# Mixture-of-experts tiles of 128 rows instead of 256, with the first weight matrices kept on chip

## The chip, the cores and the metric

The kernel runs on one core of a Trainium2 chip. The metric is the device time of one execution in microseconds (us). A kernel's time is the median of several runs. A change of under 0.3% (6.3 us here) can't be told from none.

## The reference, cut to what matters

x has 16 sequences of 256 rows with 128 channels, 4096 rows in all. A convolution with linear attention, two layers with one expert per row and three attention layers surround two calls of the layer that is changed here. `_L1_ffn_ref` picks, for each row, the two best of E = 8 experts and adds their weighted outputs:

```
xn = layernorm(x) * gamma + beta
probs = softmax(xn @ Wr + br)
scores, idx = top_k(probs, 2)
full[e] = relu(xn @ W1[e] + b1[e]) @ W2[e] + b2[e]      # W1: 128 x 512, W2: 512 x 128
sel_full = full[idx]
c[e] = relu(b1[e]) @ W2[e] + b2[e];  c_sel = c[idx];  c_total = sum of c over e
output = sum over the two of scores * (sel_full - c_sel + c_total)
return x + output
```

Everything is 32-bit floating point. The constant c_total - c_sel is prepared once, and is what a tile adds with its output.

## The kernel before, in words

The phases run one after the other: `conv_phase`, `linear_phase`, `ffn_phase`, `moe0_phase`, attention a0, `moe0_phase`, attention a1, `sparse_phase` "m1a", attention a2, `sparse_phase` "m1b". Only the sparse phases compute the layer above, each on two halves of 2048 rows (HALF = 16 blocks of P = 128 rows).

**Routing.** `routing` makes, for each half, the places of the rows sorted by expert. Each row occurs twice, so a half has 4096 rows. Each expert's rows fill tiles of SLOTS rows of their own. SLOTS is 256, MOST = 8, and TILES = 2 * MOST + E - 1 = 23 tiles are always computed. `te` holds the expert of each tile. The first half is routed inside the attention phase before. The second half is routed in the first tiles of the sparse phase, by the functions `aside` of each engine: normalised rows by ScalarE (`scaled`, L2345), transposes on TensorE (`turn_rows`), `take_rows` (L2368), `logits` (L2375), VectorE's `residual` (L2355), `biased`, `choose` (L2386 to L2429), `count` and `place` (L2466 to L2498), and `exps` (L2434). `scatter` (L2506) then writes rows to their places in DRAM by 32 indirect DMAs on POOL, of 128 rows each.

**A tile.** `sparse_phase` has Q = 46 tiles, with these steps:

- SP loads the rows (`load_rows`, L2606) and one expert's row of the DRAM table `wtab`. That row has WROW = 512 + 4 + 128 elements per partition: W1, b1 and the constant. `load` (L2614) reads the expert's number from `te` into a register (`value_load`, L2612) and puts it in the address. Both have rings of RING = 4.
- TensorE transposes the rows (`turn_in`, helper `turn`, L82), and ScalarE copies them out, scaled by gamma and beta (`take_in`, L2863).
- TensorE multiplies by W1 (`up`, L2821): four matmuls of 256 columns, in two pairs (semaphores up0 and up1). It reads the expert's number too (L2814).
- ScalarE takes the first pair through bias and relu (`relu`, L2870), VectorE the second (L2711).
- TensorE multiplies by W2 (`down`, L2832): eight matmuls of 128 columns into the single bank DN. W2e for all experts is on chip.
- VectorE adds the constant (`take_out`, L2719, semaphore y), and SP stores the tile (`store`, L2619).

A 32-bit matmul shows as two records in the trace, so `up` has 8 records and `down` 16. A transpose shows as one record.

**The order of the work** is written out by hand. On TensorE iteration q is up(q+1), turn_in(q+2), down(q), aside(q). down(q) waits for y of tile q-1, up(q+1) for xT of q+1, its weights, and the relus of q-1. On ScalarE it is relu(q+1), take_in(q+2), aside(q). On VectorE it is relu(q+1), in the second phase's second half `address(q+1)` (L2728, L2731), then take_out(q), aside(q). SP's iteration q is load_rows(q+2), store(q-4), load(q).

**Getting the results home.** The first half's outputs are gathered by POOL (`gather`, L2675, 32 indirect DMAs) and added to X by VectorE (`combine`, L2738 and L2741). gather(0) waits until all first-half tiles are stored. In m1a the second half is combined in attention a2. In m1b each second-half tile goes to DRAM array `z` in row order: `send_back` (L2683) issues one indirect DMA for 128 rows, so two a tile. POOL's order there is three gathers, then for each tile its send_backs and one gather, then the gathers that are left. After the last, SP reads z back in four sets (`load_back`, L2623, two DMAs each), VectorE runs `combine_back` on each (L2753, eight operations), and `store_out` (L2629) writes the output. The scatters of the second half wait for `down >= 8 + at // 3`, where at counts them from 0.

## Time and profile before

| | us |
|---|---|
| median of 3 runs | 2099.64 (2098.84 to 2103.7) |
| the profiled execution | 2098.11 |
| its span | 2096.4 |
| of the span: TensorE matmuls busy | 1749.2 (83%) |
| VectorE busy | 1327.0 (63%) |
| ScalarE busy | 1107.7 (53%) |
| POOL busy | 1121.1 (53%) |

Times inside the trace count from the start of the span. PE is TensorE's matmuls, PEld its weight loads, DVE VectorE, ACT ScalarE, POOL GpSimd, SP SyncE; SPq, POOLq and PEldq are those engines' queues. A row names line, engine, operation, tiles out<-in and count. "Idle before" is how long the engine had nothing to do ahead of it, and "<-" names what ended that. The two sparse phases lie at 1312 to 1500 and 1877 to 2096.

### The profile page before, as it was taken

To read this page: it belongs to the slowest core of one execution; us is meant where nothing else is said; L and a number is where in the kernel's file an instruction comes from. 1 tells how busy PE (TensorE), PEld (TensorE's weight loads), DVE (VectorE), ACT (ScalarE), POOL (GpSimd) and SP (SyncE) were. 2 spreads that over 40 slices of the span, in tenths; PEclk is the share of its full clock that TensorE was granted. 3 is DMA by queue.
4 is the path that set the end of the run, shared out by engine and by line. 5 is a ranking of instruction groups with operands and counts; after the bars stand their busy time and mean duration, and the time that the engine had idled before them with its cause. 6 is when DMAs were issued, how large, how long until landed. Compare 5 with 4: busy or idle time off the path is not lost. (4 is left out here: it accounts for less than half of the span.)

```text
span 2096.4 us, 43110 instructions
## 1 busy us (share of the span) xinstructions
PE 1749.2 (83%) x14652; PEld 1206.7 (58%) x14652; DVE 1327.0 (63%) x3888; ACT 1107.7 (53%) x2558; POOL 1121.1 (53%) x1939
## 2 busy tenths in 40 slices
PE   3979999976978788788799987899777887879994
PEld 2668888865433333344455544899534443449993
DVE  3478888845764555466778874544377788745444
ACT  2356666652654777655366655433245666564331
POOL 3145665643454555436567667255276665543475
PEclk9999999998887999989799999899868998899997
DMA  6672000000001000000000001466200000015665
GB/s 145 101 222 92 1 1 1 1 1 0 1 25 28 1 2 1 2 1 1 1 2 2 2 18 39 120 200 197 74 11 14 9 12 2 26 55 145 177 179 147
DMA packets 102402, 107.92 MB, mean 51 GB/s; under 512 B 14314, under 2 KB 81627, under 8 KB 101692
## 3 DMA queue, kind: packets, MB, share of 16 engines
q1 hardware_dynamic: 93548, 87.43, 15.9%
q0 software_dynamic: 8640, 17.74, 2.6%
q8 instruction: 121, 1.98, 0.4%
q14 instruction: 93, 0.76, 0.1%
HBM read 73.86 MB, written 36.44 MB: 53 GB/s over the span
## 5 line engine op out<-in xcount | busy, mean ns | idle before, releaser
L2147 ACT ACTIVATE a2prob<-PS 128x512 f32<-128x512 f32 x256 | 143.8, 597 | 100.9 <-PE PS L1877 100.8
L1627 DVE TENSOR_REDUCE a2mx<-PS 128x4 f32<-128x1024 f32 x128 | 155.6, 1218 | 39.1 <-PE PS L1853 38.2
L2150 ACT ACTIVATE a0prob<-PS 128x1024 f32<-128x1024 f32 x128 | 127.4, 1027 | 49.9 <-PE PS L1877 49.5
L2147 ACT ACTIVATE a1prob<-PS 128x384 f32<-128x384 f32 x256 | 116.4, 490 | 70.6 <-PE PS L1877 69.5
L1627 DVE TENSOR_REDUCE a1mx<-PS 128x6 f32<-128x768 f32 x128 | 121.9, 953 | 46.6 <-PE PS L1860 44.9
L1448 POOL TENSOR_SCALAR_AFFINE_SELECT a1prob<-a1prob 128x256 f32<-128x256 f32 x256 | 98.2, 413 | 61.5 <-ACT a1prob L2147 60.7
L2675 POOL DMA_INDIRECT gy<-rows_out,pos x64 | 61.5, 961 | 65.3 <-DMA rows_out<-m1byo 18.2
L82 PE MATMUL PS<-identb,parts 128*128 128x128 bf16 x1024 | 81.6, 229 | 14.6 <-DVE parts L1642 6.9
L2832 PE MATMUL PS<-k_W2e,m1ahid 128*128 x736 | 90.5, 276 | 0.6 <-DVE m1ayo L2719 0.6
L2832 PE MATMUL PS<-k_W2e,m1bhid 128*128 x736 | 89.8, 275 | 0.6 <-DVE m1byo L2719 0.6
L2821 PE MATMUL PS<-m1bxT,m1bwr 128*128 128x256 f32 x360 | 86.3, 382 | 4.0 <-issue 2.3
L2821 PE MATMUL PS<-m1axT,m1awr 128*128 128x256 f32 x360 | 86.2, 383 | 2.4 <-ACT m1axT L2863 1.9
L2506 POOL DMA_INDIRECT rows_in<-m1an,pos x64 | 62.3, 974 | 47.2 <-DVE pos L2498 32.3
L2832 PEld LDWEIGHTS PS<-k_W2e,m1ahid 128*128 128x128 f32 x736 | 86.6, 193 | 0.8 <-issue 0.8
L2832 PEld LDWEIGHTS PS<-k_W2e,m1bhid 128*128 128x128 f32 x736 | 85.9, 192 | 0.8 <-issue 0.8
L82 PEld LDWEIGHTS PS<-identb,parts 128*128 128x128 bf16 x1024 | 65.9, 103 | 32.6 <-issue 21.2
L2870 ACT ACTIVATE m1bhid<-PS,m1bwr 128x256 f32<-128x256 f32 x90 | 37.8, 471 | 88.1 <-PE PS L2821 87.7
L2870 ACT ACTIVATE m1ahid<-PS,m1awr 128x256 f32<-128x256 f32 x90 | 37.8, 470 | 83.8 <-PE PS L2821 83.5
L1853 PE MATMUL PS<-a2kT,a2qT 24*128 24x256 bf16 x512 | 54.6, 299 | 31.4 <-DVE a2mx L1627 28.1
L1912 PE MATMUL PS<-a2prob,va 128*32 128x256 f32 x1024 | 80.1, 437 | 0.5 <-ACT a2oT L2157 0.5
L1912 PE MATMUL PS<-a0prob,va 128*32 128x256 f32 x1024 | 74.9, 414 | 0.0
L505 POOL TENSOR_TENSOR la_ve<-la_mv,la_eps 128x2 f32<-128x2 f32 x64 | 12.6, 197 | 115.7 <-DVE la_mv L539 115.7
(539 smaller groups left out, 5190.4 us busy)
## 6 DMA issues: line engine op xcount, KB each, us to landing
m1awr<-expert_rows SPq DMA_DIRECT2D x45, 322.0 KB
m1bwr<-expert_rows SPq DMA_DIRECT2D x45, 322.0 KB
cv_im<-turned SPq DMA_DIRECT2D x48, 129.0 KB, 4.5
rows_in<-la_blank SPq DMA_DIRECT2D x46, 128.0 KB, 2.2
rows_out<-m1ayo SPq DMA_DIRECT2D x46, 128.0 KB, 1.8
m1axin<-rows_in SPq DMA_DIRECT2D x43, 128.0 KB
rows_marked<-in_blank_rows SPq DMA_DIRECT2D x23, 130.0 KB, 2.7
m1bxin<-rows_marked SPq DMA_DIRECT2D x23, 130.0 KB
```

The lines of the kernel that those rows point to most:

```text
L82: return nc.tensor.matmul(out, lhsT=in_, rhs=ident, start=True, stop=True, is_transpose=True)
L1448: last = pool.affine_select(out=part, in_=part, compare_op=ALU.is_ge, fill=0.0, base=0, pattern=[[0, NT], [1, P]], channel_multiplier=-1)
L1627: v.tensor_reduce(mx[:, 2 * j:2 * j + 2, :], bank[:, :, 0:SEG * seg_len].rearrange("p h (s n) -> p h s n", n=seg_len), AX.X, ALU.max).then ...
L1853: last = pe.matmul(bank[:, i, t * seg_len:t * seg_len + keys], lhsT=qT[rows, b % 2, h // S, t * P:(t + 1) * P], rhs=kT[rows, b % 4, h // S ...
L1912: last = pe.matmul(OB[RW * j:RW * (j + 1), gg % 2 * N + lo:gg % 2 * N + N], lhsT=va[:, b % 4, t, h, :], rhs=prob[:, h % RING, at:at + N - ...
L2147: act.activation(prob[:, h % RING, 0:n_prob], SB[(b * NH + h) % NSB][:, 0:n_prob], ACT.Exp, scale=scale).then_inc(s["exp"], 1)
L2150: act.activation(prob[:, h % RING:h % RING + EXPS, :], PS[:, h % NSB:h % NSB + EXPS, :], ACT.Exp, scale=scale).then_inc(s["exp"], EXPS)
L2506: pool.indirect_dma_start(xs[u], bass.IndirectOffsetOnAxis(ap=pos[:, u, k, t:t + 1], axis=0), n[:, u, t, 0:C + 2 * (back and u == 1)], Non ...
L2675: pool.indirect_dma_start(gy[:, t % GY, k, :], None, ys[0], bass.IndirectOffsetOnAxis(ap=pos[:, 0, k, t:t + 1], axis=0))\
L2821: last = pe.matmul(UP[q % 2][k][:, j * SLOTS:(j + 1) * SLOTS], lhsT=weights_of(q)[:, at:at + P], rhs=xT[:, q % 2, :], start=True, stop=True)
L2832: last = pe.matmul(DN[:, h * C:(h + 1) * C], lhsT=hid[:, q % 2, j, h * P:(h + 1) * P], rhs=W2e[:, bass.ds(e, 1), j, :].rearrange("p o c -> ...
L2870: last = act.activation(hid[:, q % 2, j, :], UP[q % 2][0][:, j * SLOTS:(j + 1) * SLOTS], ACT.Relu, bias=weights_of(q)[:, FF + j:FF + j + 1])
```

## The change

SLOTS becomes 128, so MOST = 16 and TILES = 39: 78 tiles a phase of half the rows. Rows and stores move in couples of two tiles (COUPLES = 20 a half, the last with one tile), and the rings hold four couples. W1 of all experts is read once, in attention a0, into `W1e`, which lies in the buffer HT. ScalarE copies the tile's W1 from there into `w1` (two buffers), at an address with the expert's number from a register (`take_w1`); `up` waits for that (semaphore wc). `wtab` keeps b1 and the constant, WROW = 132. ScalarE's iteration q is take_w1(q+2), relu(q+1), take_in(q+2), choice(q-1). The routing functions are called by `choice`, one tile later than `aside` did, with parts that shared a tile now in tiles of their own. Scatters wait for `down >= 13 + at // 2`. send_back has one indirect DMA a tile. load_back reads into `W1e`. The gathers and combines of the last half end inside the loop.

```
-WROW = FF + FJ + C
+WROW = FJ + C
-SLOTS = 2 * P
+SLOTS = P
+COUPLES = (TILES + 1) // 2
...
+                sp.dma_start(g["W1e"], g["wtab_in"].rearrange("e p w -> p e w")[:, :, 0:FF]).then_inc(s["vtab"], 16)
+                sp.dma_start(g["wtab"][:, :, 0:FJ], g["wtab_in"][:, :, FF:FF + FJ]).then_inc(s["vtab"], 16)
...
+        w1 = sb("w1", [P, 2, FF])
+            zy = [g["W1e"][:, 2 * i:2 * i + 2, :].rearrange("p k (t c) -> p k t c", t=GR) for i in range(SETS)]
...
+            for c in range(RING, CQ):
+                if c + 2 < CQ and not COUPLES <= c + 2 < COUPLES + 2:
+                    load_rows(c + 2)
+                if not returned(c - RING):
+                    store(c - RING)
+                for q in tiles_in(c):
+                    load(q)
+                if c == COUPLES - 1:
+                    load_rows(COUPLES)
+                    load_rows(COUPLES + 1)
...
-                pool.wait_ge(s["down"], 8 + at // 3)
+                pool.wait_ge(s["down"], 13 + at // 2)
                 route.scatter(pool, 1, at // 2, at % 2)
...
                 for q in range(TILES, Q):
                     send_back(q)
-                    if q < Q - 2:
+                    if q - TILES + FIRST < 2 * HALF:
                         gather(q - TILES + FIRST)
...
+            def choice(k):
+                if 1 <= k <= GROUPS:
+                    route.residual(v, k - 1)
+                if k >= 20 and k % 2 == 0 and k < 20 + 2 * GROUPS:
+                    route.residual(v, GROUPS + (k - 20) // 2)
+                if 1 <= k <= GROUPS:
+                    route.biased(v, GROUPS + k - 1, M2)
+                if k == 4:
+                    route.choose(v, 1, 0)
+                if k == 5:
+                    route.choose(v, 1, 1)
+                if k == 6:
+                    route.choose(v, 1, 2)
+                if k == 7:
+                    route.choose(v, 1, 3)
+                if k == 8:
+                    route.count(v, 1)
+                if k == 10:
+                    route.place(v, 1, 0, M)
+                if k == 11:
+                    route.place(v, 1, 1, M)
...
-                for h in range(T2):
-                    for j in range(FJ):
-                        last = pe.matmul(DN[:, h * C:(h + 1) * C], lhsT=hid[:, q % 2, j, h * P:(h + 1) * P],
+                for j in range(FJ):
+                    last = pe.matmul(DN[:, 0:C], lhsT=hid[:, q % 2, j, :],
...
+            def take_w1(q):
+                u, i = divmod(q, TILES)
+                if i == 0:
+                    act.wait_ge(o["te"], u + 1)
+                e = act.value_load(te[0:1, u, i:i + 1], min_val=0, max_val=E - 1)
+                finished(act, s["up1"], q - 2)
+                act.activation(w1[:, q % 2, :], W1e[:, bass.ds(e, 1), :].rearrange("p o w -> p (o w)"), ACT.Copy)\
+                   .then_inc(s["wc"], 1)
...
+            take_w1(0)
             take_in(0)
+            take_w1(1)
             relu(0)
+            take_in(1)
             for side in range(2):
                 route.scaled(act, GROUPS, side)
-            take_in(1)
             for q in range(Q):
+                if q + 2 < Q:
+                    take_w1(q + 2)
                 if q + 1 < Q:
                     relu(q + 1)
                 if q + 2 < Q:
                     take_in(q + 2)
-                aside(q)
+                if 1 <= q < 2 * HALF:
+                    choice(q - 1)
```

## Rows read from the trace of the kernel before

**Rows 1.** Stretch, us; busy (x) of PE, PEld, DVE, ACT, POOL; granted clock, DMA share, GB/s.
```profile
1342.00:1500.00 158.00, 155.36 (x1087) 144.42 (x1085) 76.76 (x213) 57.03 (x123) 61.06 (x64) 1.00 0.60 173
1985.00:2066.00 81.00, 79.33 (x545) 72.97 (x545) 39.94 (x126) 27.78 (x60) 61.72 (x64) 1.00 0.59 165
```

**Rows 2.** Chain that ended last, one tile of the second phase (start us, us, what).
```profile
1966.44 1.73 PE PS L2821 x8
1968.17 0.22 PE PS L82 x2
1968.39 1.79 PE PS L2832 x16
```

**Rows 3.** First sparse phase, timeline: iteration 0 on PE, last take_out.
```profile
1319.88 2.40 PE L2821 MATMUL PS<-m1axT,m1awr 128*128 128x256 f32 x7 [1.91 <-ACT m1axT L2863]
1498.67 0.42 DVE L2719 TENSOR_TENSOR m1ayo<-PS,m1awr 128x256 f32<-128x256 f32 x1 [2.23 <-PE PS L2832]
```

**Rows 4.** Second sparse phase, timeline: iterations 0 and 23 on PE, weight loads.
```profile
1885.14 1.59 PEld L2821 LDWEIGHTS PS<-m1bxT,m1bwr 128*128 128x128 f32 x8 [1.97 <-ACT m1bxT L2863]
1977.57 1.60 PEld L2821 LDWEIGHTS PS<-m1bxT,m1bwr 128*128 128x128 f32 x8
```

**Rows 5.** ACT and DVE by line: min/median/max ns of each shape.
```profile
L2147 ACT ACTIVATE a1prob<-PS x256: 464/489/535, 1018.1 to 1297.9; 128x384 f32<-128x384 f32 x128
L2147 ACT ACTIVATE a2prob<-PS x256: 579/597/655, 1534.6 to 1868.9; 128x512 f32<-128x512 f32 x128
L2870 ACT ACTIVATE m1ahid<-PS,m1awr x90: 458/469/476, 1321.0 to 1493.7; 128x256 f32<-128x256 f32 x90
L2863 ACT ACTIVATE m1axT<-PS,k_beta,k_gamma x46: 547/564/567, 1313.5 to 1490.7; 128x256 f32<-128x256 f32 x46
...
L2711 DVE TENSOR_SCALAR m1ahid<-PS,m1awr x90: 473/477/486, 1322.7 to 1494.6; 128x256 f32<-128x256 f32 x90
```

**Rows 6.** Register loads of PE's and SP's queue by line, same columns.
```profile
L2814 PEldq TENSOR_LOAD <-m1bte x46: 297/308/1017, 1877.5 to 2058.2; - x46
L2612 SPq TENSOR_LOAD <-m1bte x45: 263/273/365, 1877.5 to 2051.5; - x45
```

**Rows 7.** SP's timeline: a store, then a weight load.
```profile
1940.79 0.36 SPq L2619 DMA_DIRECT2D rows_out<-m1byo  x1
1941.90 0.36 SPq L2614 DMA_DIRECT2D m1bwr<-expert_rows  x1
```

**Rows 8.** Timeline of the last two tiles: a `down` with nothing ahead of it.
```profile
2063.86 0.42 DVE L2719 TENSOR_TENSOR m1byo<-PS,m1bwr 128x256 f32<-128x256 f32 x1 [0.53 <-PE PS L2832]
2064.42 2.05 PE L2832 MATMUL PS<-k_W2e,m1bhid 128*128 x16 [0.60 <-DVE m1byo L2719]
2066.51 0.42 DVE L2719 TENSOR_TENSOR m1byo<-PS,m1bwr 128x256 f32<-128x256 f32 x1 [1.58 <-PE PS L2832]
```

**Rows 9.** Timeline of the second half's routing on ACT and DVE.
```profile
1897.05 1.64 ACT L2345 ACTIVATE m1bn<-X,m1bshift,m1bscale 128x128 f32<-128x128 f32 x4
1899.65 0.78 ACT L2368 ACTIVATE m1bnT<-PS,k_beta,k_gamma 128x512 f32<-128x512 f32 x1 [0.97 <-PE PS L82]
1917.11 0.28 DVE L2414 SCALAR_TENSOR_TENSOR m1bws<-m1bh,m1bpr 128x128 f32<-128x128 f32 x1
1919.37 0.23 DVE L2439 TENSOR_TENSOR m1bca<-m1bab 128x128 bf16<-128x128 bf16 x1
```

**Rows 10.** POOL's timeline: first gather, last send_back, last gather.
```profile
1983.77 1.00 POOL L2675 DMA_INDIRECT gy<-rows_out,pos  x1 [18.20 <-DMA rows_out<-m1byo]
2071.84 0.96 POOL L2683 DMA_INDIRECT rows_back<-m1byo,m1bdst  x1 [0.31 <-issue]
2082.11 0.94 POOL L2675 DMA_INDIRECT gy<-rows_out,pos  x1 [0.30 <-issue]
```

**Rows 11.** Timeline of the tail: load_back and the first combine_back.
```profile
2074.18 2.03 SPq L2623 DMA_DIRECT2D m1bhid<-rows_back  x4
2078.67 2.32 DVE L2753 SCALAR_TENSOR_TENSOR X<-m1bhid,s,X 128x128 f32<-128x128 f32 x8
```

More of the change, by code:

```diff
@@ L431, in sb @@
             return ctx.enter_context(nc.sbuf_tensor("la_" + name, shape, dt))
-        blank = sb("blank", [P, SLOTS // P * C])
+        blank = sb("blank", [P, C])
         half = sb("half", [P, NT])
@@ L2522, in sparse_phase, with couple, place_in, tiles_in @@
     back = out is not None
-    COMBINE = TILES + 4
+    COMBINE = TILES + 8
     FIRST = 3
     SETS = HALF // GR
-    def returned(q):
-        return back and q >= TILES
-    def landed(eng, q):
-        if returned(q):
-            eng.wait_ge(s[f"b{(q - TILES) % RING}"], 32 * ((q - TILES) // RING + 1))
+    def couple(q):
+        return q // TILES * COUPLES + q % TILES // 2
+    def place_in(q):
+        return q % TILES % 2
+    def tiles_in(c):
+        first = c // COUPLES * TILES + c % COUPLES * 2
+        return range(first, min(first + 2, (c // COUPLES + 1) * TILES))
+    def returned(c):
+        return back and c >= COUPLES
+    def landed(eng, c):
+        if returned(c):
+            sent = sum(len(tiles_in(k)) for k in range(COUPLES, c + 1) if k % RING == c % RING)
+            eng.wait_ge(s[f"b{c % RING}"], 16 * sent)
         else:
-            eng.wait_ge(s[f"y{q % RING}"], 16 * (q // RING + 1))
+            eng.wait_ge(s[f"y{c % RING}"], 16 * (c // RING + 1))
     with ExitStack() as ctx:
-        s = semaphores(nc, ctx, name, "w0 w1 w2 w3 x0 x1 x2 x3 xt xT up0 up1 ra rv "
-                                      "down y y0 y1 y2 y3 g0 g1 g2 g3 g4 g5 cm1 cm stored"
+        s = semaphores(nc, ctx, name, "w00 w01 w10 w11 w20 w21 w30 w31 x0 x1 x2 x3 xt xT up0 up1 ra rv "
+                                      "down wc y y0 y1 y2 y3 g0 g1 g2 g3 g4 g5 cm1 cm stored"
                                       + " b0 b1 b2 b3 side dst z0 z1 z2 z3 zm1 zm" * back)
@@ L2696, in _ @@
                     send_back(q)
-                    if q < Q - 2:
+                    if q - TILES + FIRST < 2 * HALF:
                         gather(q - TILES + FIRST)
-                for at in range(Q - 2 - TILES + FIRST, 2 * HALF):
-                    gather(at)
             else:
@@ L2785, in _ @@
                     relu(q + 1)
-                if returned(q + 1) and q + 1 < Q:
+                if q + 1 < Q and returned(couple(q + 1)):
                     address(q + 1)
@@ L2790, in _ @@
             if back:
-                combine(HALF - SETS - 1)
                 for i in range(SETS):
-                    combine(HALF - SETS + i)
                     combine_back(i)
-            else:
-                for t in range(Q - COMBINE, HALF):
-                    combine(t)
         @block.tensor
@@ L2803, in turn_in @@
                 finished(pe, s["xT"], q - 1)
-                for h in range(T2):
-                    last = turn(nc, XT[:, h * P:(h + 1) * P], rows_of(q)[:, h, 0:C], ident[:, :])
-                last.then_inc(s["xt"], 1)
+                turn(nc, XT[:, 0:P], rows_of(q)[:, 0:C], ident[:, :]).then_inc(s["xt"], 1)
             expert = {}
```

205 lines of the change are left out of this document (100 added, 105 removed).

## The prediction

> **What bounds the kernel now.** I began with the busy time by stretch. Both sparse phases run at the full granted clock (the upper of the two levels, 2.4 GHz), and TensorE is busy for nearly all of each [rows 1]. In the second phase's second half POOL is busy too: 61.72 of 81 us, 64 operations whose gaps of 0.30 us are its own issue [rows 1, 10]. The chain of waits then gives a tile exactly: 1.73 for `up`, 0.22 for two transposes, 1.79 for `down`, and the next tile starts at once [rows 2]. That is 3.74 us for 256 rows (3.735 over many tiles), all TensorE. The exception is the end. From the first gather at 1983.77 to the last send_back at 2071.84 POOL starts 70 indirect DMAs back to back, one per 88.07 / 69 = 1.276 us. Three a tile make 3.83 us, just over TensorE's 3.74 [rows 10]. So the first phase and the first half of the second are TensorE's; the rest is POOL's.
>
> **TensorE's new tile.** A record of `down`, 128 columns, takes 1.79 / 16 = 0.112 us [rows 2]. The new `up` has records of just that form: 8 x 0.112 = 0.90. `down` has 8 instead of 16: 0.90. One transpose is 0.11. Sum 1.90 us for 128 rows, no better per row than 3.74 for 256 (3.80). The gain is in the rows: 78 x 128 = 9984 are computed instead of 46 x 256 = 11776, because the padding of an expert's last tile is halved. A phase would go from 46 x 3.735 = 171.8 to 78 x 1.90 = 148.2.
>
> **Whether the others keep up with 1.90.** Four loops have to close in that time.
>
> VectorE to TensorE through the single bank DN: down(q) waits for take_out(q-1). The last two tiles show that loop alone. From take_out to take_out it is 2066.51 - 2063.86 = 2.65 us, with 0.14 from the end of take_out to `down` [rows 8]. New: less 8 records (0.90), less the 0.13 that 128 fewer columns save on VectorE (at about 1 ns a column, an estimate from a pair of relus at 0.48 each for 256 [rows 5]). That leaves 1.62, under 1.90. VectorE's own work is two relus of some 0.34, take_out 0.29 and at times a combine, about 1.7 in the fullest tile.
>
> ScalarE, which gets the copy: the two prob shapes give (597 - 489) / 128 = 0.84 ns a column, so 0.60 for the copy's 512 [rows 5]. A relu becomes 0.47 - 0.11 = 0.36, take_in 0.56 - 0.11 = 0.46. Four ACTIVATEs in a row take 1.64, so each overlaps the next by about 0.09 [rows 9, 5]. Start to start: copy 0.51, relus 0.27 + 0.27, and take_in to the next copy. Between these two stands the register load, which no row shows on ScalarE. Its price on TensorE's queue is 0.31 (up to 1.02), on SP's 0.27 [rows 6]. With range check and address the whole sequence on SP takes 1941.90 - 1940.79 - 0.36 = 0.75 [rows 7]. From below it hides under take_in (0.37), and the loop is 1.42. From above it begins after take_in has ended and holds up the copy and all behind it: 0.46 + 0.75 + 0.60 + 0.63 = 2.44. I take the sequence as starting with take_in, because on TensorE, which has a register load in every tile too, the chain shows no gap for it: its queue runs ahead of a busy engine [rows 2, 6]. So: 0.75 + 0.51 + 0.54 = 1.80. That fits under 1.90, by only 0.10, and I take 1.92 per tile for it.
>
> By a page of the Trainium skill (DMA: Bandwidth & Descriptors, section "Latency and other measured facts") a register load has a floor of about 600 ns. By that rule the loop would be some 0.3 longer and the total about 2101. The rows disagree, at 0.31 and 0.27 on two other engines; no row shows ScalarE.
>
> SP: a couple costs store 0.36 and row load 0.46 plus two weight loads at 1.11, some 3.0 of 3.84 us. POOL's scatters: 32 x 1.28 = 41 us from tile 13, and 26 tiles are 50 us, so rows of tile 39 are there just in time. Either is hidden; if not, a microsecond or two at the half's boundary. DMA volume falls by far (a weight row of 132 elements in place of 644), but DMA is on no chain above, so I give nothing for it. The 2 MB read of W1 and more, smaller blank stores lie in earlier phases beside their work: nothing.
>
> **Start and routing tiles.** At the phase's start take_in(1) now comes ahead of four `scaled`, and up(0) is half as long. Iteration 0 starts 2.6 us earlier (a sum of 1.64 and half of up(0), less the copy). Then come the routing tiles. Before, they and the rest cost over the plain pace 179.2 - 171.8 = 7.4 us in the first phase (from 1319.88 to 1499.09 [rows 3]), and 92.4 - 85.9 = 6.5 in the first half of the second [rows 4]. After, ScalarE has no slack in them. Three tiles get 1.55 + 0.7 each for `scaled` and take_rows [rows 9], 2.3 each in place of TensorE's 1.27: 6.9. The first group after take_in(1) delays copy and relu by 2.4. exps waits for VectorE, some 2. VectorE's `choose` parts, up to 2.26 (1917.11 to 1919.37 [rows 9]) against a slack of about 1, give 3. In sum 14.2.
>
> **First phase:** -2.6 + 78 x 1.92 - 171.8 + 14.2 - 7.4 = -17.8.
>
> **Second phase.** First half: -2.6 + 39 x 1.92 - 85.9 + 14.2 - 6.5 = -5.9. Then POOL. Before, gather(0) came 1983.77 - 1977.57 = 6.2 after iteration 23 began [rows 4, 10]. SP's store of the last tile stands behind a row load that waits for address(24). Now it stands behind address(42), two short iterations further: 3.8 + 1.1 + 1.0 + 0.5 for SP + 2.5 to land = 8.9, so +2.7. POOL's work to the last send_back is 39 + 32 = 71 starts in place of 70 (eight gathers came after it before): +1.3. TensorE is ahead by then, at 1.92 against POOL's 2.55 a tile. Tail: before, 22.2 from load_back at 2074.18 to the span's end, held by the last gather at 2082.11 and the combines after it [rows 10, 11]. Now all combines are done. The fourth set lands about 11.5 after the start (the eight issues take 6.3, an estimate from the start at 2074.18 and 0.5 to 1 us each), combine_back 2.3 [rows 11] and the last store 4.2 make 18.0: -4.2. Sum -6.1.
>
> Longer `place` in two attention phases (39 tiles for 23): +0.8 at most.
>
> **Total** -17.8 - 6.1 + 0.8 = -23.1 on the profiled execution's 2098.11: 2075.0. The median of the runs is 1.5 above that execution, so 2076.5.
>
> **The rivals.**
> (B) ScalarE's loop sets the pace. The register sequence is 0.3 longer than SP's, as TensorE's worst loads are, so 2.13 per tile. For: a margin of 0.10, and the load is new on this engine. Against: SP's narrow 263/273/365 ns [rows 6]. 117 tiles x 0.21 = +24.6: 2101, no change. The rule of the Trainium skill named above says this too. Chance 0.14.
> (C) Slower: the register load waits for ScalarE to finish, the upper bound of 2.44. TensorE, DN and relus then wait on wc in every tile. +0.52 x 117 = 61: 2137. POOL's half would stay at 2.55. It turns from gain to loss at 1.92 + 23.1 / 117 = 2.12 per tile. Against: on TensorE the load is hidden in every tile [rows 2]. Chance 0.13, milder forms near 2115 among it.
> (D) The change is not only TensorE's: SP or the scatters come late at the halves' boundaries, three us at each of two boundaries, and small waits make the pace 1.98 (+7): 2089. Chance 0.10.
> (E) Routing tiles cost as before: 14.2 becomes 8, twice: 2064. Chance 0.08.
> The forecast has 0.55.
>
> **How the numbers follow.** Faster by over 0.3% (under 2093.3; 0.3% is about what a measurement can tell from no change): forecast, D, E and a part of B, 0.77. Within: 0.09. Slower: 0.14. The range goes from E's 2061 up to B's 2102 and leaves C out.
>
> **What would show it.** TensorE's tiles 1.90 to 1.95 apart, 0.112 per record of both matmuls; ScalarE's copy at 0.60 with under 0.1 idle ahead of it and near 95% busy; 39 tiles per half; POOL from 8 to 9 us after the half's last iteration without waits; last combine before load_back. If take_w1 is what TensorE waits for, and the pace is over 2.1, the forecast falls.

## The result and the profile after

The changed kernel takes 2071.63 us (median of 3 runs, 2067.91 to 2076.66) where the kernel before took 2099.64. The ratio is 0.9883, 95% interval [0.9852, 0.9915]. The forecast was 2076.5, in a range of 2061 to 2102, so the median came 4.9 us below it. The profiled execution took 2076.66, the longest of the three, where 2075.0 was forecast.

The page of the changed kernel: its span, busy times, and TensorE's granted clock in 40 slices.
```profile
span 2074.8 us, 46088 instructions
...
PE 1720.9 (83%) x14912; PEld 1194.3 (58%) x14912; DVE 1351.2 (65%) x4112; ACT 1224.9 (59%) x2906; POOL 1112.0 (54%) x1932
...
PEclk9989999999897999989699999899958899899998
```
ScalarE is busy 117 us more than before, of which the copy is 98 (156 x 0.63). TensorE's matmuls are busy 28 us less.

Windows of the changed kernel in the two sparse phases, columns as in [rows 1]:
```profile
1325.00:1490.00 165.00, 161.25 (x1368) 157.28 (x1368) 96.95 (x351) 131.37 (x331) 74.35 (x107) 0.98 0.42 117
...
1953.00:2050.00 97.00, 83.79 (x681) 78.90 (x679) 55.06 (x229) 63.24 (x158) 64.30 (x66) 0.98 0.41 111
```
The first phase is still TensorE's (161 of 165 us). In the second phase's second half TensorE now has 13 us of 97 free, and ScalarE is busy for 131 of 165 us in the first phase (80%), far from full. (The granted clock of 0.98 against the 1.00 of [rows 1] is the phase's start, which this window takes in: it is 0.50 over 1320 to 1330, and 1.00 from 1340 to 1380.)

The chain that ended last, one tile of the changed kernel, answers to [rows 2]:
```profile
1926.23 0.90 PE PS L2844 x8
1927.12 0.11 PE PS L83
1927.23 0.89 PE PS L2855 x8
```
That is the forecast's 0.90 + 0.11 + 0.90 to the hundredth, 0.112 a record.

**Phases.** To see where the time went I cut each trace at the barriers between phases (VectorE's DRAIN at each). Attention a1 and a2 hold no instruction that the change adds except longer `place` steps. The stretch of 0.9 us between m1a and a2 is left out. All profiles of this study, those of unchanged code too, in us:

```
profile              a1     m1a    a2     m1b
before              316.0  190.0  374.3  218.3
before, again       316.1  191.6  366.2  217.3
changed             325.1  172.2  368.2  210.3
changed, again      315.0  169.2  374.9  210.0
e1_early_load       316.5  169.5  371.3  209.2
e4_double_load      322.6  180.1  367.1  213.8
e5_gathers_last     325.1  170.9  363.2  208.1
e6_w1_by_dma        324.9  178.0  366.6  213.6
e7_onchip_256       314.9  189.6  371.3  217.8
e8_routing_as_before 315.1 175.8  364.8  214.5
e9_sends_first      318.6  171.4  362.3  208.2
e10_all             315.0  169.6  367.0  203.4
e11_two_queues      316.1  169.6  367.1  204.8
e12_fixed_w1        315.1  169.3  374.4  209.8
```
The first pair of profiles alone would mislead: a1 is 9.1 longer after the change and a2 6.1 shorter. Neither is the change's, as the rows below show. The sparse phases, by contrast, repeat to within 3 us. m1a has unchanged code in four profiles of the changed kernel's kind (the two, e5, e9), 169.2 to 172.2, mean 170.9, against a mean of 190.8 in two profiles before: -19.9 (forecast -17.8). m1b goes from 217.8 to 210.15: -7.65 (forecast -6.1). Together -27.5.

### The profile page after: what moved, and what is told of

Read it like the earlier page. It is cut to its first block and busy times, and to the rows that moved or that the text cites. A ratio compares the mean times of both kernels' runs of the same rounds, so it can differ in the third digit from the quotient of the medians.

```text
span 2074.8 us, 46088 instructions
## 1 busy us (share of the span) xinstructions
PE 1720.9 (83%) x14912; PEld 1194.3 (58%) x14912; DVE 1351.2 (65%) x4112; ACT 1224.9 (59%) x2906; POOL 1112.0 (54%) x1932
## 3 DMA queue, kind: packets, MB, share of 16 engines
q8 instruction: 125, 2.05, 0.4%
## 5 line engine op out<-in xcount | busy, mean ns | idle before, releaser
L2699 POOL DMA_INDIRECT gy<-rows_out,pos x64 | 61.0, 953 | 60.0 <-DMA rows_out<-m1byo 16.2
L2844 PE MATMUL PS<-m1bxT,m1bw 128*128 128x128 f32 x624 | 88.2, 286 | 5.8 <-ACT m1bxT L2887 4.0
L2844 PE MATMUL PS<-m1axT,m1aw 128*128 128x128 f32 x624 | 86.9, 283 | 5.0 <-ACT m1axT L2887 3.9
L2855 PEld LDWEIGHTS PS<-k_W2e,m1bhid 128*128 128x128 f32 x624 | 77.5, 195 | 16.4 <-issue 16.0
L2508 POOL DMA_INDIRECT rows_in<-m1an,pos x64 | 62.4, 975 | 42.4 <-DVE pos L2500 27.5
L2855 PE MATMUL PS<-k_W2e,m1ahid 128*128 x624 | 83.6, 277 | 1.0 <-DVE m1ayo L2743 0.9
L2844 PEld LDWEIGHTS PS<-m1bxT,m1bw 128*128 128x128 f32 x624 | 78.8, 198 | 9.7 <-ACT m1bxT L2887 4.9
L2844 PEld LDWEIGHTS PS<-m1axT,m1aw 128*128 128x128 f32 x624 | 77.5, 195 | 8.1 <-ACT m1axT L2887 4.8
L2855 PEld LDWEIGHTS PS<-k_W2e,m1ahid 128*128 128x128 f32 x624 | 76.7, 194 | 1.8 <-issue 1.7
L2734 DVE TENSOR_SCALAR m1ahid<-PS,m1awr 128x128 f32<-128x128 f32 x154 | 46.9, 346 | 42.8 <-PE PS L2844 38.8
```

The costliest lines, as they stand in the source:

```text
L2508: pool.indirect_dma_start(xs[u], bass.IndirectOffsetOnAxis(ap=pos[:, u, k, t:t + 1], axis=0), n[:, u, t, 0:C + 2 * (back and u == 1)], Non ...
L2699: pool.indirect_dma_start(gy[:, t % GY, k, :], None, ys[0], bass.IndirectOffsetOnAxis(ap=pos[:, 0, k, t:t + 1], axis=0))\
L2734: last = v.tensor_scalar(hid[:, q % 2, j, :], UP[q % 2][1][:, (j - HJ) * SLOTS:(j - HJ + 1) * SLOTS], weights_of(q)[:, j:j + 1], 0.0, ALU. ...
L2844: last = pe.matmul(UP[q % 2][k][:, j * SLOTS:(j + 1) * SLOTS], lhsT=w1[:, q % 2, at:at + P], rhs=xT[:, q % 2, :], start=True, stop=True)
L2855: last = pe.matmul(DN[:, 0:C], lhsT=hid[:, q % 2, j, :], rhs=W2e[:, bass.ds(e, 1), j, :].rearrange("p o c -> p (o c)"), start=(j == 0), st ...
```

## The experiments

In this section "ratio" is against the kernel before, run beside it on the same chip, with its 95% interval. Cuts in the edits are marked "...".

**The same kernels again.** No edit.

> No edit: the changed kernel once more, for what its phases do from one profile to another. Theory R: the 9 us by which attention a1 was longer in the first profile of the changed kernel, and the 6 us by which a2 was shorter, are not the change's: they move from profile to profile with the clock granted to TensorE there. Then a1 comes out anywhere from 314 to 327 us and a2 from 366 to 376, while the sparse phases stay within 1 us of 172.2 and 210.3. Rival: the change itself lengthens a1 (39 places in place of 23, smaller blank stores, W1 on chip): 325 again, within 1 us. Total 2068 to 2077.

Measured: 2061.67 us against 2096.38, ratio 0.9841 [0.9797, 0.9885]; a1 315.0, m1a 169.2, a2 374.9, m1b 210.0.

> No edit: the kernel before once more, with a profile, as the other half of the comparison of phases. So far its only profile has a1 316.0, m1a 190.0, a2 374.3, m1b 218.3 us, and two profiles of the changed kernel have a1 325.1 and 315.0, a2 368.2 and 374.9. Theory R: attention phases move by several us from profile to profile in both kernels, and the sparse phases by one: m1a 189 to 191, m1b 217 to 219.5. Rival: the kernel before moves less than the changed one, or its sparse phases move by 3 or more, and then the gain by phases can't be read from single profiles.

Measured: 2094.56, ratio 0.9988 [0.9968, 1.0008]; a1 316.1, m1a 191.6, a2 366.2, m1b 217.3.

One window over attention a1, the changed kernel, the same again, and the kernel before (columns as in [rows 1], one fence per kernel):
```profile
995.00:1321.00 326.00, 279.87 (x3363) 166.18 (x3363) 231.99 (x583) 178.32 (x391) 216.26 (x458) 0.89 0.03 10
```
```profile
998.00:1312.00 314.00, 266.79 (x3362) 159.18 (x3363) 230.04 (x583) 178.33 (x391) 214.86 (x457) 0.94 0.03 10
```
```profile
995.00:1310.00 315.00, 269.81 (x3362) 160.68 (x3363) 229.43 (x583) 178.34 (x391) 215.41 (x458) 0.93 0.03 11
```
The number of matmuls (3362 or 3363) and ScalarE's busy time are the same in all three. Only the granted clock differs, 0.89 against 0.94 and 0.93, and TensorE's busy time with it, 13 us between the first two. At the phase's start the first profile has a clock of 0.50 (the lower level, 1.2 GHz) for a whole stretch of 24 us where the other has 0.66:
```profile
996.00:1020.00 24.00, 15.62 (x81) 8.02 (x82) 11.05 (x33) 3.77 (x6) 11.33 (x20) 0.50 0.00 1
```
```profile
996.00:1020.00 24.00, 12.89 (x86) 6.35 (x86) 11.30 (x34) 4.15 (x7) 12.72 (x21) 0.66 0.00 1
```
All 14 profiles say the same. Where a1's granted clock is 0.94 it takes 314.9 to 315.1 us, at 0.93 316.0 to 316.5 (both with tiles of either size), at 0.89 324.9 to 325.1; a2 takes 374.3 to 374.9 at 0.83, 371.3 at 0.84 and 362.3 to 368.2 at 0.85 to 0.88. Theory R holds: with no edit a1 moves by 10.1 us and a2 by 6.7 between two profiles of the changed kernel, and a2 by 8.1 between two of the kernel before. The bounds on the sparse phases were too narrow: m1a of the changed kernel moved by 3.0 where 1 was expected, m1a of the kernel before by 1.6. The changed kernel's median of 2061.67 also came out below the expected 2068 to 2077. Its five executions had a granted clock of 0.918 to 0.924 over the whole span, where the first three had 0.915 to 0.920. From here on the sparse phases are compared, and a difference in m1a of under 3 us is taken as none unless its cause shows.

**Tiles of 256 rows, W1 on chip.** From the kernel before:
```
-WROW = FF + FJ + C
+WROW = FJ + C
...
-                        last = pe.matmul(UP[q % 2][k][:, j * SLOTS:(j + 1) * SLOTS], lhsT=weights_of(q)[:, at:at + P],
+                        last = pe.matmul(UP[q % 2][k][:, j * SLOTS:(j + 1) * SLOTS], lhsT=w1[:, q % 2, at:at + P],
...
+                if q + 2 < Q:
+                    take_w1(q + 2)
```


> Edit, from the kernel before: W1 on chip and copied per tile by ScalarE, weight rows of 66 KB, but the tiles keep 256 rows and the routing its old steps. Theory P (the gain is the halved padding alone): nothing that bounds a tile of 3.74 us has changed, the copy of 0.6 us hides in ScalarE's free time, DMA volume was on no chain: m1a 189 to 191 us, m1b 217 to 219, total that of the kernel before within 2 us. Rival M: the weight loads held something up, in the second half above all, where POOL's indirect transfers share the engines with them: m1b shorter by 3 us or more.

Measured: 2089.38 us against 2094.62, ratio 0.9981 [0.9967, 0.9994]; m1a 189.6, m1b 217.8. Its window over 158 us of m1a, to be read against the first row of [rows 1]:
```profile
1342.00:1500.00 158.00, 154.54 (x1080) 143.56 (x1079) 76.53 (x213) 80.72 (x161) 60.93 (x64) 1.00 0.39 109
```
The DMA share falls from 0.60 to 0.39, ScalarE gets 24 us more to do, and the phases stay as they were (190.0 and 191.6, 218.3 and 217.3 before). The total came out 5.2 us lower, more than the 2 expected, but the ratio's 0.2% is under the 0.3% that can be told from none. Theory P holds at 256 rows: transfers were on no chain, and W1 on chip by itself is worth nothing in the two phases.

**Tiles of 128 rows, W1 by DMA.** From the changed kernel:
```
-WROW = FJ + C
+WROW = FF + FJ + C
...
-                                         lhsT=w1[:, q % 2, at:at + P],
+                                         lhsT=weights_of(q)[:, at:at + P],
...
-                if q + 2 < Q:
-                    take_w1(q + 2)
```


> Edit: tiles of 128 rows as after the change, but W1 comes with each tile's weight row from memory as before the change (330 KB a tile in place of 66 KB), and ScalarE copies nothing. Theory W (the change needs its first part): a tile then moves 330 + 64 + 64 KB; in 1.93 us that is 237 GB/s, above all that the page of the kernel before shows in a fortieth of its span (177 GB/s), so transfers set the pace, at 458 KB / 177 = 2.6 us or more: m1a 171 + 65 x 0.65 = some 210 us or more, m1b longer too, total 2100 to 2150. Rival V: the queues deliver it, and ScalarE's copy was not needed: m1a 169 to 172, total the changed kernel's, or a little less because ScalarE is free.

Measured: 2080.14, ratio 0.9934 [0.9909, 0.9959]; m1a 178.0, m1b 213.6. Between the two theories. Its window of m1a:
```profile
1325.00:1490.00 165.00, 158.52 (x1338) 154.20 (x1338) 92.69 (x327) 82.30 (x248) 70.76 (x96) 0.98 0.79 232
```
And what TensorE waited for in m1a (who waited <- what it waited for: us in total, times, longest):
```profile
PE PS L2842 <- DMA m1awr<-expert_rows: 3.4, 4, 1.9
```
The queues delivered 232 GB/s over the phase. The 177 GB/s on which theory W rested was no ceiling, and not even the most that the page of the kernel before shows: its slices in m1a go up to 200, and one early in the span is at 222. But the weights came late four times, 3.4 us in all, most of it at the half's boundary (three tiles there took 9.7 us, 5.8 in the changed kernel), and the plain tiles of m1a's first half came at 2.02. Late weights are not all of that pace. Three of the slow tiles there (2.29, 2.26 and 2.26 us) had a register load of 0.54 to 0.66 us on TensorE's queue, in place of 0.30; why the load took longer, and why m1b's first half kept a pace of 1.94, stay open. So W1 on chip is worth 7.1 us in m1a and 3.5 in m1b, by one profile: some two fifths of the gain. The rest comes with the tiles of 128 rows and the orders changed with them, which no run takes apart (the next one shows that part of it is the routing's order). The two parts belong together: W1 on chip gains nothing at 256 rows and some 10 us at 128.

**The routing in its old steps.** From the changed kernel:
```
-                if 1 <= q < 2 * HALF:
-                    choice(q - 1)
+                choice(q)
...
                 if k == 5:
                     route.choose(v, 1, 1)
+                    route.choose(v, 1, 2)
                 if k == 6:
-                    route.choose(v, 1, 2)
+                    route.choose(v, 1, 3)
+                    route.count(v, 1)
...
-                if k == 9:
+                if k == 7:
                     route.ranks(pe, 1, M)
...
-            take_in(1)
             for side in range(2):
                 route.scaled(act, GROUPS, side)
+            take_in(1)
```


> Edit, from the changed kernel: the second half's routing goes back to its old places, one tile earlier, with choose 1 and 2, choose 3 and count, both places in one tile each, ranks two tiles earlier, and the first four scaled ahead of take_in(1). Theory C: with tiles of 1.9 us VectorE has about 1 us of slack in a tile, and the joined parts (2 x 2.3 us and more) hold up take_out twice over, so the single steps are worth 2 to 4 us a phase, and take_in(1) behind the scaled 1.6: m1a 174 to 177 where the changed kernel had 169 to 172, m1b 214 to 216. Rival: VectorE's work is the same in sum and only spread; TensorE waits the same time in fewer tiles: within 1.5 us of the changed kernel in both phases.

Measured: 2081.91, ratio 0.9938 [0.9915, 0.9961]; m1a 175.8, m1b 214.5. Waits of TensorE over the routing tiles, this kernel (to 1365) and the changed one (to 1370):
```profile
PE PS L2840 <- ACT m1axT L2882: 4.5, 2, 3.0
PE PS L2454 <- DVE m1acb L2447: 1.9, 1, 1.9
```
```profile
PE PS L2844 <- ACT m1axT L2887: 3.9, 3, 1.8
```
Theory C's numbers hold, and one of its two mechanisms. From the phase's start to `up(1)` it took 8.4 us here and 5.95 in the changed kernel: 2.4 for take_in(1) behind four `scaled`. Behind `up(1)` one tile took 4.43 us (3.58 in the changed kernel) and one 4.81, where the changed kernel's longest is 3.70. In the tile of 4.81 TensorE waited 1.9 us in `ranks` (L2454) for VectorE's `count`, which stands here behind `choose` 3 in one tile. The wait of `down` for take_out that the theory had is not in the list. The single steps and the new order at the start are worth 4.9 and 4.3 us a phase together; the run doesn't part the steps from the shift by one tile.

**ScalarE's room.** From the changed kernel:
```
+                act.value_load(te[0:1, u, i:i + 1], min_val=0, max_val=E - 1)
                 e = act.value_load(te[0:1, u, i:i + 1], min_val=0, max_val=E - 1)
```


> Edit: take_w1 reads the expert number twice, one register load more on ScalarE per tile; nothing else. It measures what a register load costs on ScalarE's queue and how much room ScalarE has. Theory S (the forecast's model): the sequence starts with take_in, lasts 0.65 us and shows 0.28 of it as idle time ahead of the copy; a second load adds 0.3 to 0.55 us (load, check of the range) that nothing covers, ScalarE's loop of about 1.87 becomes 2.2 to 2.4, and it sets the pace: +0.25 to +0.45 over some 78 tiles (the second half stays POOL's), +20 to +35 us, 2092 to 2107. Rival H: the load is hidden under ScalarE's work or costs under 0.1: no more than 2075.

Measured: 2081.4, ratio 0.9937 [0.9905, 0.997]; m1a 180.1, m1b 213.8; plain tiles 2.05 apart. ScalarE's timeline in the changed kernel, where each copy (L2896) shows 0.18 us of idle time ahead of it, and then with the second load:
```profile
1416.81 0.46 ACT L2887 ACTIVATE m1axT<-PS,k_beta,k_gamma 128x128 f32<-128x128 f32 x1
1417.45 0.63 ACT L2896 ACTIVATE m1aw<-HT 128x512 f32 x1 [0.18 <-issue]
1418.32 0.62 ACT L2904 ACTIVATE m1ahid<-PS,m1awr 128x128 f32<-128x128 f32 x2 [0.24 <-PE PS L2844]
1418.83 0.46 ACT L2887 ACTIVATE m1axT<-PS,k_beta,k_gamma 128x128 f32<-128x128 f32 x1
1419.47 0.63 ACT L2896 ACTIVATE m1aw<-HT 128x512 f32 x1 [0.18 <-issue]
```
```profile
1415.96 0.46 ACT L2887 ACTIVATE m1axT<-PS,k_beta,k_gamma 128x128 f32<-128x128 f32 x1
1417.33 0.63 ACT L2897 ACTIVATE m1aw<-HT 128x512 f32 x1 [0.91 <-issue]
...
1418.36 0.46 ACT L2887 ACTIVATE m1axT<-PS,k_beta,k_gamma 128x128 f32<-128x128 f32 x1
1418.96 0.63 ACT L2897 ACTIVATE m1aw<-HT 128x512 f32 x1
```
In the changed kernel the copy starts 0.64 us after take_in, whose own 0.46 hide most of the register sequence. With two sequences it starts 1.37 us after it in one tile, but 0.60 in the next, where the first load was taken up ahead of the last relu, 0.58 us before take_in. Neither theory's number came out: the second load adds 0.54 us to the queue (from the start of the first to the start of the second), and costs 0.1 us a tile, not 0.25 to 0.45, since ScalarE's queue makes up part of it in every other tile. But it isn't hidden either. So ScalarE has some room and less than 0.54 us of it; the run doesn't measure the forecast's margin of 0.10.

**TensorE's register load earlier.** The changed kernel's tiles come 1.89 and some 2.03 apart by turns in long stretches. From the changed kernel:
```
-            def up(q):
+            def load_expert(q):
...
+            def up(q):
...
                     up(q + 1)
                 if q + 2 < Q:
+                    load_expert(q + 2)
                     turn_in(q + 2)
                 down(q)
```


> Edit: TensorE reads the expert number of tile q+2 into its register before it waits for take_out(q-1) in down(q), in place of after down(q); nothing else. Theory Q (the queue loop): after the change a pair of tiles takes 3.92 us because the register load of tile q+2 stands in TensorE's queue behind down(q)'s wait for take_out(q-1), so up(q+2) can't start before that take_out + 1.4 us. With the load ahead of that wait the pace goes from a mean of 1.96 to TensorE's own 1.90: over the 65 or so plain tiles of the first phase and the first half of the second -4 to -5 us, the second half staying POOL's: about 2067. Rival N: the pairs of 1.89 and 2.03 come from something else (VectorE's take_out late in every other tile, or ScalarE's copy): pace unchanged, 2071 to 2072.

Measured: 2063.8, ratio 0.9852 [0.981, 0.9894], not to be told from the changed kernel's 0.9841; m1a 169.5, m1b 209.2. Weight loads of `up` in the changed kernel, then here, a few tiles of each:
```profile
1417.52 0.97 PEld L2844 LDWEIGHTS PS<-m1axT,m1aw 128*128 128x128 f32 x8
...
1419.41 0.97 PEld L2844 LDWEIGHTS PS<-m1axT,m1aw 128*128 128x128 f32 x8
...
1421.36 0.97 PEld L2844 LDWEIGHTS PS<-m1axT,m1aw 128*128 128x128 f32 x8
...
1423.25 0.97 PEld L2844 LDWEIGHTS PS<-m1axT,m1aw 128*128 128x128 f32 x8
...
1425.43 0.74 PEld L2844 LDWEIGHTS PS<-m1axT,m1aw 128*128 128x128 f32 x6 [0.21 <-issue]
```
```profile
1417.06 0.97 PEld L2846 LDWEIGHTS PS<-m1axT,m1aw 128*128 128x128 f32 x8
...
1419.07 0.97 PEld L2846 LDWEIGHTS PS<-m1axT,m1aw 128*128 128x128 f32 x8
...
1420.97 0.97 PEld L2846 LDWEIGHTS PS<-m1axT,m1aw 128*128 128x128 f32 x8
```
The alternation is gone here and in the three later kernels with this edit, as theory Q says. Without the edit it comes and goes: it is absent for long stretches of m1a in e2_after_again and of m1b in e9_sends_first. In the first half of m1b the plain tiles come at 1.897, where four profiles without the edit have 1.924, 1.930, 1.936 and 1.902. In the first half of m1a they come at 1.93, where those four have 1.966, 1.916, 1.939 and 1.948. So the queue loop is real but costs 0 to 3 us a phase, because it only bites when the two tiles fall into that order. My 4 to 5 us came from one profile in which they mostly did, and the 3.0 us between the changed kernel's two profiles of m1a lie in these tiles: from `up(1)` to the last `up` it took 160.2 and 157.2 us.

**The single slow tiles.** Some tiles of m1a stay slow: 13 of the 60 plain ones take 1.98 to 2.13 us. (In the first half of m1b none is over 1.91.) From e1_early_load, with the expert's number gone from ScalarE, so that every tile computes with W1 of expert 0:
```
...
-                e = act.value_load(te[0:1, u, i:i + 1], min_val=0, max_val=E - 1)
...
-                act.activation(w1[:, q % 2, :], W1e[:, bass.ds(e, 1), :].rearrange("p o w -> p (o w)"), ACT.Copy)\
+                act.activation(w1[:, q % 2, :], W1e[:, 0, :], ACT.Copy)\
```


> Edit, from e1_early_load: ScalarE copies W1 of expert 0 for every tile, at a fixed address, without a register load (so all tiles compute with W1 of expert 0). e1_early_load still has single tiles of 1.98 to 2.1 among those of 1.90. Theory A: they are ScalarE's, whose loop of about 1.87 leaves 0.03 and falls behind when a relu comes late; without the load its loop is about 1.5, and plain tiles come at 1.90 throughout: m1a 167 to 168.5, and the routing tiles, where ScalarE has no slack at all, shorter by 0.3 to 0.6 us each. Theory B: they are VectorE's or the records' own: m1a 169 to 170 as in e1_early_load.

Measured: 2067.28, ratio 0.9852 [0.9834, 0.9871]; m1a 169.3, m1b 209.8, plain pace 1.93 as in e1_early_load. Theory A falls: ScalarE's register load costs nothing in plain tiles. The 15 intervals of the routing tiles took 39.4 us in place of 40.0, together, not each. What makes these tiles 0.1 longer stays open.

**POOL's order.** From the changed kernel, e5_gathers_last:
```
                 for q in range(TILES, Q):
                     send_back(q)
-                    if q - TILES + FIRST < 2 * HALF:
+                    if q - TILES + FIRST < 2 * (HALF - SETS):
                         gather(q - TILES + FIRST)
+                for at in range(2 * (HALF - SETS), 2 * HALF):
+                    gather(at)
```


> Edit: the last eight gathers (four row tiles) and their combines go behind the last send_back, as in the kernel before, in place of ahead of it; store_out(0,3) goes next to last. Theory T: POOL's queue bounds the second half, and the end waits for the last send_back + 17.4 us of load_back, combine_back and store. With 8 starts of 1.276 us taken from ahead of it, the last send_back comes up to 10 us earlier, unless TensorE is met first: it makes 39 tiles in 75 us from the half's start, POOL's 63 starts end some 8.9 + 80.4 = 89 us after it, so POOL still bounds. The eight gathers take 10.2 us and land while load_back runs; the end then waits for the later of both chains, 10.2 + 2 for landing + combines and a store of 5: about the same 17.4. Gain 7 to 10 us: 2062 to 2065. Rival K: the eight transfers slow load_back or hold combine_back behind the combines in VectorE's order, and half or all of the gain is given back: 2068 to 2072.

Measured: 2063.72, ratio 0.986 [0.9819, 0.99]; m1b 208.1, so 2.1 us gained where theory T had 7 to 10. (The total lies in theory T's range, but a2 takes 363.2 us in this profile, at a clock of 0.88.) Timeline of the end:
```profile
2037.67 0.96 POOL L2708 DMA_INDIRECT rows_back<-m1byo,m1bdst  x1 [0.96 <-DVE m1byo L2746]
...
2039.30 0.96 POOL L2708 DMA_INDIRECT rows_back<-m1byo,m1bdst  x1 [0.66 <-DVE m1byo L2746]
...
2046.09 0.35 DVE L2765 SCALAR_TENSOR_TENSOR X<-gy,s,X 128x128 f32<-128x128 f32 x1 [7.07 <-DMA gy<-rows_out,pos]
```
The last send_back came 182.6 us after the phase's first `up`, where the changed kernel has 188.8 and 188.5: 6 us earlier, not 10. At the end POOL waits for take_out (0.96 and 0.66 us above). That TensorE is late by then because the full ring held it back earlier in the half is my reading, not shown. And the four pairs of combines stand on VectorE between the combine_backs, so the stretch from the last send_back to the end grew from 19.8 to 23.8 us. Rival K took two thirds.

Then e9_sends_first:
```
-    FIRST = 3
+    FIRST = 5
...
-                for at in range(FIRST):
-                    gather(at)
                 for q in range(TILES, Q):
                     send_back(q)
-                    if q - TILES + FIRST < 2 * HALF:
-                        gather(q - TILES + FIRST)
+                    if FIRST <= q - TILES < 2 * HALF + FIRST - 0:
+                        gather(q - TILES - FIRST)
```


> Edit, from the changed kernel: POOL issues the first six send_backs of the second half before gather(0), then a gather after each (gather(k) behind the send_back of tile k+5 of the half), and VectorE's combines move eight tiles later to match, the last two behind the loop. Theory G: POOL stands still for some 7 us ahead of gather(0), while rows of the half's first tiles are already waiting to be sent, and TensorE later stops on the full ring; gather(0) comes some 3 us later (the sixth send_back waits for its tile), but only 65 of the 71 starts are left behind it: 83 us, last send_back 3 us earlier, m1b 206 to 208 us against 210.3 and 210.0; m1a unchanged at 169 to 172. Rival: the combines behind the loop and the later stores give it back, m1b 209.5 to 211.

Measured: 2063.92, ratio 0.9847 [0.9817, 0.9877]; m1b 208.2. The last send_back came 185.6 us after the phase's first `up` (188.8 and 188.5 in the changed kernel): 3.0 us earlier, as forecast. The stretch behind it grew from 19.8 to 20.9 us, so 1.9 us are left. Theory G's mechanism holds; its range for m1b, 206 to 208, was missed by 0.2.

And e9_sends_first together with e1_early_load, e10_all: e9's loop with four gathers behind it in place of e5's eight, load_expert, and
```
+                ahead = COUPLES <= c < COUPLES + RING
+                if ahead:
+                    store(c - RING)
                 if c + 2 < CQ and not COUPLES <= c + 2 < COUPLES + 2:
                     load_rows(c + 2)
```


> Edits, from the changed kernel: TensorE's register load one tile earlier (as in e1_early_load), the send_backs first (as in e9_sends_first), SP's last four stores of the first half ahead of the row loads in their iterations, and the last four gathers (not eight) behind the last send_back. Expected from the sum of what each showed or should show: m1a 169 to 170.5, first half of m1b -1.4, gather(0) no longer waits for the store, last send_back some 9 us earlier (about 180 us after the first up, where the changed kernel has 188.8 and 188.5), the end 1 us of combines more than that: m1b 201 to 204, total 2052 to 2058 if the attention phases are as in the mean of the others, and 0.3 to 0.5% below the changed kernel in any case. Rival: TensorE bounds the half's end, as the waits of POOL for take_out in e5_gathers_last hint, and m1b stays at 206 or more.

Measured: 2060.68 against 2098.26, ratio 0.9814 [0.9789, 0.9838]; m1a 169.6, m1b 203.4. POOL at the second half's start in the changed kernel, then here:
```profile
1965.60 1.00 POOL L2699 DMA_INDIRECT gy<-rows_out,pos  x1 [16.20 <-DMA rows_out<-m1byo]
```
```profile
1943.21 0.96 POOL L2712 DMA_INDIRECT rows_back<-m1byo,m1bdst  x1 [10.14 <-DVE m1byo L2748]
...
1953.35 0.96 POOL L2712 DMA_INDIRECT rows_back<-m1byo,m1bdst  x1 [0.94 <-DVE m1byo L2748]
1954.61 1.00 POOL L2704 DMA_INDIRECT gy<-rows_out,pos  x1 [0.30 <-issue]
```
POOL stood still for 16.2 us there before, and for 10.1 now. m1b is 6.7 us shorter than the changed kernel's, within the forecast of 201 to 204, and the last send_back stands at 180.7. The total, 2060.68, missed its range of 2052 to 2058. Its ratio is 0.3% and 0.7% under the changed kernel's two (0.9841 and 0.9883). The first one's interval overlaps its own, the second one's doesn't: the gain is shown in the phase, and in the total it is likely.

**The tail's issue.** From e10_all, load_back's second loads on ScalarE's queue:
```
-                for k in range(2):
-                    sp.dma_start(zy[i][:, k], zrows[k, i]).then_inc(s[f"z{i}"], 16)
+                sp.dma_start(zy[i][:, 0], zrows[0, i]).then_inc(s[f"z{i}"], 16)
...
+                for i in range(SETS):
+                    act.dma_start(zy[i][:, 1], zrows[1, i]).then_inc(s[f"z{i}"], 16)
```


> Edit, from e10_all: of the eight loads of load_back four are issued by ScalarE's queue, four by SP's. Theory V (the tail is VectorE's): in the changed kernel combine_back waits 0.25 us in all after its first set has landed and then works without a gap, so faster issue can only bring the first set earlier, by the second load's 0.65 us: m1b shorter by 0.3 to 1 us. Theory I, the forecast's reading of the tail (the fourth set lands 11.5 us after the start because eight issues take 6.3): 3 us shorter.

Measured: 2055.29, ratio 0.9796 [0.9776, 0.9817]; m1a 169.6, m1b 204.8. The start of the tail with one queue, then with two:
```profile
2033.63 5.06 SPq L2645 DMA_DIRECT2D HT<-rows_back  x8
...
2037.79 4.54 DVE L2782 SCALAR_TENSOR_TENSOR X<-HT,s,X 128x128 f32<-128x128 f32 x16 [10.59 <-DMA HT<-rows_back]
```
```profile
2032.56 2.03 SPq L2644 DMA_DIRECT2D HT<-rows_back  x4
2032.58 2.12 ACTq L2950 DMA_DIRECT2D HT<-rows_back  x4
...
2037.26 4.54 DVE L2781 SCALAR_TENSOR_TENSOR X<-HT,s,X 128x128 f32<-128x128 f32 x16 [11.28 <-DMA HT<-rows_back]
```
The issue takes 2.1 us in place of 5.1, but the first combine_back starts 4.70 us after it in place of 4.16. From the last send_back to the end it took 21.6 us (21.0 with one queue), so the tail is not shorter and theory I falls. The rest of m1b's 1.4 us more lies ahead of the tail, where this edit does nothing: from `up(1)` to the half's second tile it took 88.5 us (86.9). Theory V's reading (VectorE without a gap behind its first set) stands, though its small gain didn't show either. The run's ratio is the lowest of all, but m1b gives no reason for it, and its interval overlaps that of e10_all.

## Why the prediction was right, step by step

**TensorE's tile: right.** 0.112 a record in both matmuls, a tile of 1.90. In the first halves the plain tiles came at 1.916 to 1.966 in m1a and 1.902 to 1.936 in m1b, where I took 1.92. The 0.02 stood for ScalarE's thin margin. What it paid for was, in large part, TensorE's own queue. The register load for tile q+2 stands behind down(q)'s wait for take_out(q-1), and `up(q+2)` starts 1.43 us after that take_out has ended (1416.09, then 1417.52; e1_early_load removes it). The take_out, and TensorE's register loads in the changed kernel:
```profile
1415.80 0.29 DVE L2743 TENSOR_TENSOR m1ayo<-PS,m1awr 128x128 f32<-128x128 f32 x1 [0.34 <-PE PS L2855]
...
L2837 PEldq TENSOR_LOAD <-m1ate x78: 296/302/595, 1322.6 to 1487.0; - x78
```
I had listed four loops and missed this fifth one, which takes 3.92 us for two tiles, so 1.96. It also lets a slow register load through: in this profile's m1a nine of the 60 plain tiles follow a load of 0.40 to 0.595 us, and they took 2.13 us on average, where the 50 with a load under 0.33 took 1.93. The forecast had the load hidden on TensorE in every tile, which at 3.74 us a tile it was. That 1.92 fitted so well is in part luck: the margin that I priced cost little, and the loop that I missed cost about as much.

**The four loops: right.** DN and take_out: the last two take_outs of m1a are 1.63 apart, forecast 1.62. The changed kernel's timeline:
```profile
1490.03 0.29 DVE L2743 TENSOR_TENSOR m1ayo<-PS,m1awr 128x128 f32<-128x128 f32 x1 [0.22 <-PE PS L2855]
...
1491.66 0.29 DVE L2743 TENSOR_TENSOR m1ayo<-PS,m1awr 128x128 f32<-128x128 f32 x1 [1.33 <-PE PS L2855]
```
ScalarE: the copy takes 0.63 (forecast 0.60), relus 0.62 for two, take_in 0.46. Two of the forecast's signs did not come: the copy has 0.18 us of idle time ahead of it (under 0.1 was expected), and ScalarE is busy for 80% of the phase, not near 95%. The register load, new on this engine, and the copy in the changed kernel (columns as in [rows 5]):
```profile
L2894 ACTq TENSOR_LOAD <-m1ate x78: 272/278/576, 1322.6 to 1485.3; - x78
...
L2896 ACT ACTIVATE m1aw<-HT x78: 612/630/649, 1323.9 to 1486.0; 128x512 f32 x78
```
0.278 us stands beside the 0.27 of SP and 0.31 of TensorE from which it was estimated [rows 6]. The floor of about 600 ns that the Trainium skill gives (DMA: Bandwidth & Descriptors, section "Latency and other measured facts") is not what this read shows. Rival B needed 0.3 us more. It gave as its ground TensorE's worst loads, but 1.02 us [rows 6] is 0.7 above SP's 0.27, not 0.3. e4_double_load, which adds 0.54, cost 13 us in the two phases, so 0.3 more would hardly have brought 24.6: the queue takes up a load early in every other tile. Rival C (the load waits for ScalarE to finish) is ruled out by the copy starting 0.64 us after take_in starts, and by e12_fixed_w1: no load, no gain. Rival D's late boundary didn't come: the three tiles around m1a's took 5.7 to 5.8 us in the changed kernel. It came with W1 by DMA (9.7).

**Start and routing: close.** The phase's start to `up(1)` fell from 8.5 to 5.95 and 6.0: -2.5 (forecast -2.6). From `up(1)` to the last `up` m1a's four profiles have a mean of 158.96 us: 76 x 1.92 + 13.0, where I had 14.2. (Its four parts sum to 14.3; how much each cost was not measured.) Before, the same stretch held 8.3 over the plain pace, the mean of two profiles, not 7.4. These two make the 2.1 us by which m1a came out better. Rival E (routing costs as before) is not what happened.

**The second half: right.** gather(0) came 8.8 us after the half's second `up` began (forecast 8.9). From it to the last send_back 71 starts took 89.5 us (89.3). The timeline of the changed kernel's end, to be read against [rows 11]:
```profile
2055.08 0.96 POOL L2707 DMA_INDIRECT rows_back<-m1byo,m1bdst  x1 [0.30 <-issue]
...
2057.42 5.38 SPq L2645 DMA_DIRECT2D HT<-rows_back  x8
2061.26 2.31 DVE L2777 SCALAR_TENSOR_TENSOR X<-HT,s,X 128x128 f32<-128x128 f32 x8 [9.18 <-DMA HT<-rows_back]
...
2063.83 6.76 DVE L2777 SCALAR_TENSOR_TENSOR X<-HT,s,X 128x128 f32<-128x128 f32 x24 [0.25 <-DMA HT<-rows_back]
```
The tail from load_back to the span's end took 17.4 (forecast 18.0), but not for the reason given. I let the fourth set's landing decide, 11.5 us after the start. The rows show VectorE at work without a gap from 2063.83 on: after the second set it is VectorE's 2.3 us a set.

**The parts given nothing.** W1 on chip was costed by its copy alone, and the fall in DMA volume at nothing. At 256 rows that is so (e7). At 128 rows, which is where the change uses it, the volume does count: e6 loses 10.6 us. The sum was right since the change has both parts, but "DMA is on no chain above" was read from the old tile only. The single routing steps, too, were a cost in my sum (14.2) without the other side: the old steps and the old order at the start would have cost 4.9 more. And the 0.8 us for longer `place` steps didn't show: at the same clock of 0.94, a1 takes 315.0 and 315.1 us with 39 tiles (e2_after_again, e12_fixed_w1) and 314.9 with 23 (e7_onchip_256).

**The total.** -27.5 in the two phases by repeated profiles, against -23.9. The runs gave -28.0 and -34.7. The 7 us between these two are of the size by which the attention phases move, and go with the granted clock (medians of 0.916 and 0.923 over the span); that all of it lies there is not shown, since only one execution of each has a trace. So the total's closeness to the forecast, 4.9 us, is partly luck as well; the phases are what the sum was right about, to 3.6 us.

## What to carry to other kernels

When a tile gets smaller, list the loops anew, and put each engine's own queue among them: an instruction that could run early (a register load) is worth nothing behind a wait that comes late. Test each "hidden" at the new pace, not the old one: the same weight rows that cost nothing at 3.7 us a tile cost 10 us at 1.9. And before reading a gain out of two profiles, cut both at the same barriers and repeat each: here untouched phases moved by 10 us and the changed ones by 1 to 3.

## What the runs showed of the hardware

A register load from on-chip memory takes 0.28 us on ScalarE (median of 78, at most 0.58). With its range check it is 0.51 us, and the copy starts 0.64 us after the load does, all but 0.18 of it beside the engine's own work. On TensorE's queue the same load takes 0.30, and up to 0.60. A queue took up such a load while its engine still worked (the load and take_in start together on ScalarE). Behind down(q)'s wait it came late: in the changed kernel `up` follows take_out by 1.43 us, and with the load ahead of the wait (e1_early_load) the alternation that came of it is gone. The DMA queues of this core delivered 232 GB/s over 165 us in e6_w1_by_dma, with up to 316 in 4 us. And the clock granted to TensorE in one and the same attention phase was 0.89 in one profile and 0.94 in another, 10 us apart for 3363 matmuls each, with no edit between them.
